# A two-layer decoder block on one core: order changes at four stage borders, and gates of a routed feed-forward stage laid out by transfers

## The reference, cut to what matters

```python
comb = jnp.sum(jax.nn.one_hot(indices, N_ROUTED, dtype=x.dtype) * weights[..., None], axis=1)
h = jax.nn.silu(g) * u              # g, u: token, expert, 64
h = h * comb[:, :, None]            # one gate per token and expert
out = out + jnp.einsum('tem,emd->td', h, wd_r)
```

## Time and profile before

| | us |
|---|---|
| median of three runs | 1560.12 |
| lowest and highest of them | 1559.51, 1562.1 |
| the profiled execution's own time | 1562.81 |
| its span (first to last instruction) | 1560.8 |

### The profile page before, as it was taken

One profiled execution on the slowest core, in us unless ns is written; L12 is line 12 of the kernel. 1 busy time (PEld: TensorE's weight loads), 2 busy tenths in 40 slices (PEclk: granted clock), 3 DMA queues, 4 the chain that ended last, 5 costly groups with the idle time before them and its releaser, 6 DMA issues.

```text
span 1560.8 us, 28560 instructions
## 1 busy us (share of the span) xinstructions
PE 1514.9 (97%) x10996; PEld 1316.0 (84%) x11018; DVE 988.6 (63%) x2131; ACT 729.8 (47%) x1874; POOL 203.7 (13%) x215
## 2 busy tenths in 40 slices
PE   7999999899999999999999999999998999999997
PEld 6898988789999999978888867777766988999886
DVE  6777777864554555576666567788886464444547
ACT  4766666622222222223323367788884444444443
POOL 1322322310000000030000034212221300000001
PEclk9999999999999999999999999999999999999999
DMA  6000100011010101100000585677750000000001
GB/s 217 1 15 1 42 2 1 28 40 41 26 36 19 52 27 39 34 1 34 1 13 1 74 139 67 86 101 134 105 79 28 1 28 28 28 27 27 27 0 54
DMA packets 43080, 66.50 MB, mean 43 GB/s; under 512 B 4576, under 2 KB 33504, under 8 KB 42848
## 3 DMA queue, kind: packets, MB, share of 16 engines
q1 hardware_dynamic: 42976, 65.09, 20.0%
HBM read 36.24 MB, written 2.10 MB: 25 GB/s over the span
## 4 chain that ended last, share of the span: by engine, by line
PE 90%; DVE 6%; ACT 2%; issue 1%; DMA 1%; POOL 0%; SPq 0%; DVEq 0%; POOLq 0%; ACTq 0%
PE ps L85 23%; PE ps L86 22%; PE ps L87 22%; PE ps L1859 3%; PE ps L1873 3%; PE ps L1849 2%; PE ps L392 2%; PE ps L404 2%; PE ps L417 2%; PE ps L1904 2%; PE ps L1887 1%; ACT wPr L472 1%; PE ps L1846 1%; PE ps L1895 1%; PE ps L1823 0%
## 5 line engine op out<-in xcount | busy, mean ns | idle before, releaser
L858 ACT ACTIVATE m2hT_h<-ps 128x512 fp32r<-128x512 f32 x128 | 76.7, 599 | 281.4 <-PE ps L87 281.4
L982 DVE TENSOR_TENSOR m6hT_l<-m6h,m6hT_h 128x512 fp32r<-128x512 f32 x128 | 88.5, 691 | 169.5 <-ACT m6hT_h L856 169.5
L984 DVE SCALAR_TENSOR_TENSOR m2hT_l<-ps,m2hT_h 128x512 fp32r<-128x512 f32 x128 | 88.4, 691 | 163.4 <-ACT m2hT_h L858 163.4
L855 ACT ACTIVATE m6h<-ps,m6b 128x512 f32<-128x512 f32 x128 | 88.4, 691 | 202.5 <-PE ps L87 196.2
L1985 ACT ACTIVATE nPr<-ps,negm 128x128 f32<-128x128 f32 x512 | 147.2, 383 | 26.2 <-DVE negm L2088 25.3
L87 PE MATMUL ps<-w_h,m6hT_l 128*128 128x256 f32 x512 | 144.4, 282 | 0.0
L85 PE MATMUL ps<-w_h,m6hT_h 128*128 128x256 f32 x512 | 143.0, 279 | 0.7 <-DVE m6hT_l L982 0.7
L86 PE MATMUL ps<-w_l,m6hT_h 128*128 128x256 f32 x512 | 143.6, 280 | 0.0
L87 PE MATMUL ps<-m2w_h,m2hT_l 128*128 128x256 f32 x448 | 126.8, 283 | 0.0
L86 PE MATMUL ps<-m2w_l,m2hT_h 128*128 128x256 f32 x448 | 126.7, 283 | 0.0
L85 PE MATMUL ps<-m2w_h,m2hT_h 128*128 128x256 f32 x448 | 126.3, 282 | 0.0
(11 more groups left out here) (322 smaller groups left out, 4323.6 us busy)
## 6 DMA issues: line engine op xcount, KB each, us to landing
nKm<-nKc_h SPq DMA_DIRECT2D x64, 128.0 KB, 4.5
nQs<-nQc_h SPq DMA_DIRECT2D x64, 128.0 KB, 5.7
raw<-in_w_e1i SPq DMA_DIRECT2D x9, 512.0 KB, 3.2
raw<-in_w_e1o SPq DMA_DIRECT2D x9, 512.0 KB, 3.3
raw<-in_w_e6i SPq DMA_DIRECT2D x9, 512.0 KB, 3.3
raw<-in_w_e6o SPq DMA_DIRECT2D x9, 512.0 KB, 3.3
nKm<-nKc_l SPq DMA_DIRECT2D x32, 128.0 KB, 5.2
nQs<-nQc_l SPq DMA_DIRECT2D x32, 128.0 KB, 6.0
```

What stands on the lines that cost most here:

```text
L855: nc.scalar.activation(c.h32[:, u % 2, :], ps[:, u % 2, :], ACT.Gelu, bias=bias)
L858: nc.scalar.activation(c.hT[0][:, ch, :], ps[:, u % 2, :], ACT.Relu).then_inc(c.s["hi_ready"], 1)
L982: last = nc.vector.tensor_tensor(c.hT[1][:, ch, :], c.h32[:, u % 2, :], c.hT[0][:, ch, :].bitcast(F32), ALU.subtract)
L984: last = nc.vector.scalar_tensor_tensor(c.hT[1][:, ch, :], ps[:, u % 2, :], 0.0, c.hT[0][:, ch, :].bitcast(F32), ALU.max, ALU.subtract)
```

## The change

- **Stage 1 to 2.** ACT copies the second transposed half before it writes the first half's mask; from p = 30 both copies come before the exponentials. DVE splits the mixture's weights ahead of the step's last fill instead of behind it.
- **Stage 2 to 3.** The last combine is cut: sequence 0 of the group after the router logits, sequences 1 to 3 after the gates' copy, the norm of group 2 after product 3, the statistics after product 4, the norm of group 3 after product 5. In the first group the first down product moves behind `u` of chunk 3. The splits of stage 4's weights move from products 4 to 7 to products 5 to 8.
- **Gates.** The selector, its building and 32 `spread` matmuls go. DVE copies `combT` once, in float32, and SP issues for each group eight transfers of 256 KB, each from two rows of `combT`, repeated 64 times each, to a buffer of 128 rows. Chunks 2 to 5 have a buffer of their own, chunks 6 and 8 share one, 7 and 9 another, and SP waits for the product of chunk `c-2` before it issues 8 and 9. DVE multiplies from the buffer.
- **Stage 3 to 4.** In the last group the two query products run back to back after `u` of chunk 9, in banks of their own. SP loads `U_A5` after group 0 as before, but `U_E6` and the context only after group 1; POOL splits `U_E6` at quads 29 and 33.
- **Stages 5 to 6.** DVE does the normalisation and transposed copy ahead of the stage-6 pieces, except at quad 128; the biases are copied 14 steps earlier; part 1 of the gate steps moves one step later; at the last step the first product of stage 6 precedes the transposes; the split of `w_out` of expert 1 moves from behind hidden chunk 5 to behind chunk 6.

```diff
-            for half in range(2):
+            both = p >= W_BOTH_AT
+            for half in range(2):
                 if 0 <= p - 2 < NP:
-                    transposed_p(2 * (p - 2) + half)
+                    if half == 0 or not both:
+                        transposed_p(2 * (p - 2) + half)
+                    if half == 0 and both:
+                        transposed_p(2 * (p - 2) + 1)
+                if half == 1 and p < NP - 1:
+                    mask_behind(p, 0)
                 if p < NP:
                     exponentials(2 * p + half)
-                if p < NP - 1:
-                    act.wait_ge(s["p_exp"], 2 * p + half + 1)
-                    mask(half)
+            if p < NP - 1:
+                mask_behind(p, 1)
...
+            for kind, i in w_following(p):
+                if kind == "w":
+                    split_unit(v, c2.first, i, cut(c2.slot0, i * RAW, RAW), RAW)
             for kind, i in f[3]:
                 fill(kind, i)
...
+            if c.gelu and u == M_LATE_W + 1:
+                start.append(("w", M_LATE_W))
...
-            def last_combine():
-                normalise(NG - 2)
-                combine(E_OUT // 2 - 1, 2 * NG - 1)
-
...
-            return last_combine, lambda: stats_of(NG - 1), last_norm
+            return (lambda *seqs: combine(E_OUT // 2 - 1, 2 * NG - 1, *seqs)), lambda: normalise(NG - 2), lambda: stats_of(NG - 1), last_norm
...
-                order += ([("s", c)] if c >= SC else []) + ([("nq", 0)] if last and c == FC - 1 else []) + [("t", c)]
+                order += ([("nq", 0), ("nq", 1)] if queries else []) + [("t", c)]
+                order += [("nq evac", 0)] if queries else []
...
+    def ffn_place(c):
+
+        i = c - SC
+        return (i, 0, 1) if i < 4 else (4 + i % 2, (i - 4) // 2, 2)
+
+    def ffn_lay_gates(sp, g, chunks):
+        s = F3.s
+        if chunks[0] == SC:
+            sp.wait_ge(s["g_evac"], ffn_evac(g, FT))
+        for c in chunks:
+            i, load, _ = ffn_place(c)
+            if load:
+                sp.wait_ge(*ffn_gated(g, c - 2))
+            rows2 = F3.combT[2 * (c - SC):2 * (c - SC) + 2, :]
+            sp.dma_start(F3.gate[i], rows2.unsqueeze(1).broadcast_to([2, R_MID, GT])).then_inc(F3.laid[i], 16)
...
             sp.dma_start(F3.Xs[:, :, :], X[:, bass.ds(g * GB, GB), :]).then_inc(s["xs_loaded"], 16)
...
+            ffn_lay_gates(sp, g - 1, range(SC, FC))
+        ffn_lay_gates(sp, NG - 1, range(SC, FC))
...
-            nc.tensor.matmul(bank, F3.sel[:, c - SC, :], F3.combT[:, :], start=True, stop=True).then_inc(s["g_full"], 1)
...
-                v.wait_ge(s["g_full"], ffn_full(g, ffn_spread(g, c)))
+                i, load, loads = ffn_place(c)
+                v.wait_ge(F3.laid[i], g * (16 * loads) + 16 * (load + 1))
                 v.wait_ge(s["t_done"], g * FC + c + 3)
-                nc.vector.tensor_tensor(F3.h32[:, c % 2, :], F3.tt[:, c % 2, :], ps[:, 4 + c % 2, :], ALU.mult).then_inc(s["g_evac"], 1)
...
+                nc.vector.tensor_tensor(F3.h32[:, c % 2, :], F3.tt[:, c % 2, :], F3.gate[i], ALU.mult).then_inc(s["gated"], 1)
...
-            hi, lo = F3.combT[0:R_N, :], F3.combT[LO_ROWS:LO_ROWS + R_N, :]
-            link(nc.vector.tensor_copy(hi, src))
-            nc.vector.tensor_tensor(lo, src, hi.bitcast(F32), ALU.subtract).then_inc(s["g_evac"], 1)
+            nc.vector.tensor_copy(F3.combT[0:R_N, :], src).then_inc(s["g_evac"], 1)
...
-            order += n_quad("s", n) + shared + n_seq("zn", n, 8) + n_quad("t", n, 2)
+            back = n_seq("zn", n, 8) + n_quad("t", n, 2)
+            order += n_quad("s", n) + (shared + back if n == NQUADS else back + shared)
+            order += [("mv", 0)] if n == NQUADS - NQ + M_BIAS_AT else []
...
-    M_B_AT, M_G_AT, M_E_AT = (13,), (13, 14, 17), 17
+    M_B_AT, M_G_AT, M_E_AT, M_BIAS_AT = (13,), (13, 15, 17), 17, 2
...
-            n_sync(sp, {0: load_e6, NG + 1: load_b2})
+            n_sync(sp, {0: load_a5, 1: load_e6, NG + 1: load_b2})
...
-            n_pool(pool, {3: lambda: split_a5(0), 7: lambda: split_a5(1), 19: lambda: split_e6(0), 23: lambda: split_e6(1),
+            n_pool(pool, {3: lambda: split_a5(0), 7: lambda: split_a5(1), 29: lambda: split_e6(0), 33: lambda: split_e6(1),
```

More of the change, by code:

```diff
@@ L490, in mask, with mask_behind @@
                                  ACT.Identity).then_inc(s["masked"], 1)
+        def mask_behind(p, half):
+            act.wait_ge(s["p_exp"], 2 * p + half + 1)
+            mask(half)
         x_hi(0)
@@ L1021, in combine @@
             v.wait_ge(c.s["d_full"], i * (2 * NG) + q + 1)
-            for j in range(GB):
+            for j in seqs or range(GB):
                 t = g * GB + j
@@ L1054, in mix_vector @@
                 hidden(0, k)
-                weights(0, k)
+                if not c.gelu or k != M_LATE_W:
+                    weights(0, k)
             elif kind == "w":
@@ L1144, in program @@
     F3.h32 = m.place("f3h32", [P, 2, GT], F32)
-    F3.combT = m.place("f3combT", [P, GT], F32R)
+    F3.combT = m.place("f3combT", [P, GT], F32)
     F3.lg = m.place("f3lg", [P, GB, R_N], F32)
@@ L1154, in program @@
     F3.r = m.place("f3r", [P, GB, D], F32)
-    m2 = Region(nc, M2.end, r2.end - M2.end)
-    F3.sel32 = m2.place("f3sel32", [P, FC - SC, P], F32)
-    F3.sel = r1b.place("f3sel", [P, FC - SC, P], F32R)
+    NGT = 6
+    n_x0_at = r2.start + 45120
+    assert m.at <= n_x0_at
+    gates4 = Region(nc, n_x0_at, 8 * KB).place("f3gates4", [P, 4, GT], F32)
+    gates2 = r1b.place("f3gates2", [P, 2, GT], F32)
+    F3.gate = [gates4[:, i, :] for i in range(4)] + [gates2[:, i, :] for i in range(2)]
+    F3.laid = [sem(f"f3_laid{i}") for i in range(NGT)]
     F3.s = signals("f3", "xs_loaded xt_hi g_full g_evac soft_exp comb_ready gu_full sg_ready t_done hi_ready h_ready "
-                         "d_full r_done ln_var rstd_ready x_done sel_pool sel_ready")
+                         "d_full r_done ln_var rstd_ready x_done gated pad_ready")
     assert m.at <= n_at
-    FG = 2 + FC - SC + DC
-    LO_ROWS = 32
-    F_LINKS = 19 + 2 * GB
+    FG = 2 + DC
+    F_LINKS = 18 + 2 * GB
     def ffn_order(first, last):
@@ L1178, in ffn_order @@
                 k = [("nk", k) for k in range(DC)] if last and c == FC - 2 else []
+                queries = last and c == FC - 1
+                order += [("h", c - 1)] if queries else []
                 order += x[:1] + k[:1] + ([("nk evac", 0)] if k else []) + [("u", c)] + x[1:] + k[1:]
-                order += ([("s", c)] if c >= SC else []) + ([("nq", 0)] if last and c == FC - 1 else []) + [("t", c)]
+                order += ([("nq", 0), ("nq", 1)] if queries else []) + [("t", c)]
+                order += [("nq evac", 0)] if queries else []
             if c == SC - 1:
                 order.append(("c", 0))
-            if 2 <= c < FC:
+            if 2 <= c < FC and not (first and c == 2):
+                order += ([("d", 0)] if first and c == 3 else []) + [("d", c - 2)]
+            if c == FC:
+                order += [("nq evac", 1)] if last else [("x", k) for k in range(DC)]
                 order.append(("d", c - 2))
-            if c == FC and last:
-                order += [("nq evac", 0), ("nq", 1), ("h", c - 1), ("nq evac", 1), ("d", c - 2)]
-            elif c == FC:
-                order += [("x", k) for k in range(DC)]
-                order.append(("d", c - 2))
-            if c >= 1 and not (c == FC and last):
+            if c >= 1 and not (c == FC - 1 and last):
                 order.append(("h", c - 1))
@@ L1210, in ffn_evac @@
         return g * FG + (DC + k + 3)
[L1212 removed]
+    FL, FT, FX = 0, 1, 2
     def ffn_last(g):
```

101 lines of the change are left out of this document (42 added, 59 removed).

## The result

The changed kernel takes **1743.4 us** (median of 4 runs, 1742.2 to 1744.5) against 1561.1 of the kernel before (1559.5 to 1564.1): a ratio of 1.1165, interval 1.1145 to 1.1186. The forecast was 1531.5 with a range of 1522 to 1585. It is wrong in sign and size: the change makes the kernel 182 us slower.

The account below looks back on a forecast made before the run. PE, busy 97% of the span, bounds the kernel. Terms 7.7 + 3.3 + 5.2 + 7.0 + 5.5 = 28.7 off the profiled 1562.8 give 1534.1, less 2.7 for the median: 1531.5 us, range 1522 to 1585.

Parts of the forecast that it names:

- the low end: Gate transfers in stage 3: 0.75 us of moving each (256 KB at 341 GB/s), so gates arrive in time.
- 33 us: High end of a gate transfer's price: two source rows at the lays' 4 GB/s per row, 8 GB/s together.
- 8t + 2: Time in us for a group's eight gate transfers of t each, set against 35.1 us from copy to last gated product.
- The second rival: Stage 3 gates: transfers held by the rows read, t between 6.1 and 33 us, time above 1602; chance 0.12.
- the estimate of 9.6 us: Gate transfer's time at 27.2 GB/s for four neighbouring rows, giving a kernel time near 1700.
- The first rival: Stage 3 gates late: two source rows use 2 of 16 engines, t 5.2 or 6.1 us, time 1573 or 1602; chance 0.17.
- Stage 3 without the selector: Removing 32 spread matmuls at 0.24 us each saves 7.7 us, all on PE's path.
- "Nothing" for what stands behind SP's new waits: Loads of U_A4 and Xs behind SP's gate waits have at least two chunks of time left, costing nothing.
- Stage 1 to 2, 3.3 us: Earlier split and second copy remove 3.4 us of PE waits plus half the clock's 3.3; bounds 1 and 5.
- Stage 2 to 3, 5.2 us: Shorter combine ahead of the router closes both PE gaps, 3.5 us, plus 1.8 of half clock; bounds 3 and 5.5.
- Stage 3 to 4, 7.0 us: First queries' lays give 1.9, the issue gap 3.7, the clock 1.4; bounds 3 and 10.
- Stages 5 to 6, 5.5 us: Reordered product, biases and split give 3.5, normalisation's DVE pieces and clock 2.0; bounds 2 and 11.

Follow-up runs that it names:

- Run 1: Changed kernel with 15 transfers of different source shapes appended, each alone in the queue; 256 KB from rows 0,1 took 12.3 us, from rows 0,4 6.7.
- run 3: Changed kernel with combT copied twice, each gate transfer reading its two rows 65 apart instead of neighbours: 1589.9 us (1.0196).
- the late clearing: POOL clears nKm only after DVE's last split of stage 4's weights; border edits alone on the kernel before: 1541.5 us; changed kernel with gates through HBM: 1538.1.
- run 5: Kernel before with the border edits alone, selector and its 32 matmuls kept, first queries unmoved: 1551.3 us (0.9948).
- run 11: Changed kernel with gate transfers reading 128 rows of weights wF instead of two of combT, and nKm cleared late: 1532.7 us (0.9828).
- run 2: Changed kernel with the same 32 transfers each reading 128 rows of weights wF instead of two rows of combT: 1543.5 us (0.990).

## Why the prediction was wrong

**The gates' transfers: the step that failed.** It is the choice "I take the low end, because a read row need not be bound as a written one is". Run 1 shows that a read row is bound, at 25 to 27 GB/s, and that neighbours share the bound. The other end of that price, 33 us, was wrong as well: the value lay between, at 10.4. The rivals had the queue right: their sum 8t + 2, with t = 10.4, gives 85.2 us for a group, and 86.0 was read. The second rival (two rows read still more slowly, 0.12) came true in its place and its reason, rows read that hold the transfer: 1562.8 - 2.7 - 21.0 + 4 x (85.2 - 35.1) = 1740, and 1743.4 was measured. That it comes so near is in part luck: the borders outside stage 3 gave the changed kernel 11.9 us of the 15.8 in the sum, and stage 3 grew by less than the sum has. By the estimate of 9.6 us, worked out from the figure of the Trainium skill's page *SBUF — State Buffer* ("Door 1: The DMA port swizzle"), the same sum is 1714. The first rival's price exists too, on other rows (run 3); its reason, two engines of 16, was true of the changed kernel (share 0.12) but was not what held it. The reason given against both, that the lays crowd at their written end, said nothing of reads out of few rows. No row before showed such reads. The remark that the trace shows 27.2 GB/s "for writes at most" has no row either: by the prediction's own count the lays' 128 GB/s over 32 written rows is 16 for each four.

**Stage 3 without the selector.** 7.7 was forecast. With the late clearing, stage 3 is 189.2 us with the selector and 182.4 without, 6.8 less: right within 1 us. (The two kernels also differ in the place of the first queries' products.) "Nothing" for what stands behind SP's new waits was right only with quick transfers: in the changed kernel PE waited 6.4 us for a load of `Xs`.

**Stage 1 to 2, 3.3 us.** 3.1 measured (683.9 to 680.8), but not by the path described. PE's waits for the second copy went from 4.3 us to 0.6; in their place stand 2.0 for the mask written back (L489) and 1.1 for POOL, so 4.2 us of the 30 are still idle where 5.0 were the earlier trace rows. What fits the gain is the clock, 0.89 to 1.00, by the prediction's own sum worth (1 - 0.89) x 30 = 3.3, of which it had counted half. The gap was passed on, the half clock was not.

**Stage 2 to 3, 5.2 us.** Both gaps of the earlier trace rows went. In the changed order stage 3 is nevertheless 6.6 us longer with the selector (199.7 in run 5) where it should be 5.2 shorter, by a cost the working never named: the sentence on what the moves release looked at SP and at PE's order, not at POOL, for which `stage_done` is the start of a clearing. Without the collision stage 3 with the selector is 3.9 us shorter than before (193.1 to 189.2): inside the bounds 3 to 5.5.

**Stage 3 to 4, 7.0 us.** 1.3 from the last SiLU to the first exponential and 5.5 over the exponentials: 6.8. PE's wait of 3.7 for issue is gone; the lays of the first queries still cost 1.9 of their 2.6.

**Stages 5 to 6, 5.5 us.** 388.0 to 379.6 is 8.4, inside 2 to 11. Where 7.9 us of 60 were idle, 1.8 are, and the clock is 1.00 for 0.94. The term counted 3.5 for the gaps and 2.0 for the clock. The gaps closed by 6.1, and the clock is worth up to 3.6 by the same sum; both were taken too low.

**The sum** of the terms was 28.7; run 11, which has what the forecast priced, is 29.0 shorter in its span. That these agree within 0.3 us is in part luck: stage 3 gave 10.7 of its 12.9, the end 8.4 for 5.5. The sum was sound but for two costs: the two-row source, priced at its low end with no row beneath it and worth 200 us, and the clearing beside the split, not in it at all and worth 10.8.

## What to carry to other kernels

Before a broadcast by DMA from few SBUF rows, ask which rows: here row 0 alone, rows 0 and 1, or rows 0 to 3 gave 25 to 27 GB/s together, with two engines or sixteen; spread the sources, or store the few KB to HBM and load the rows from there (1.6 + 3.5 us here). A signal that is moved moves everything it releases: list each engine that waits for it, and what of another engine will then run beside that work. A long clearing on GpSimd held a float32 copy or multiplication from SBUF to SBUF on VectorE for its whole length, and the profile shows it as an operation that is some 20 times too long, not as a wait.

## What was not expected of the hardware

- Row 0 repeated 128 times keeps 16 engines 0.89 busy for 27 GB/s; rows 0 and 4 move 51 GB/s with 0.13. A high DMA share is no sign of bandwidth.
- Issuing can block: SP's issues of gates lasted 0.5 us at the least, 4.1 in the median and 10.6 at most, and 0.6 in the median with the wide source (run 2), so what stands behind slow transfers in SP's order starts late too.

```profile
L1254 SPq DMA_DIRECT2D f3gates<-f3combT x32: 514/4093/10575, 685.5 to 1054.7; - x32
```

- After the clearing of `nKm` the next one, of `nV`, held DVE again (a split of weights took 2.23 us for 0.56). Clearings are not the only case, and the kernel before has it too. There a norm (L2066, 0.40 us in the median) took 2.18 from 942.08, beside POOL's split of weights (L703, 2.37 us from 941.74). And a DVE operation on two SBUF tiles (L572, 0.29 us in the median) took 1.26 from 129.68, beside a sum of POOL that also reads SBUF (L310, 1.34 us from 129.44). Whether a clearing cut in small pieces would let DVE in between was not tried.
